# Another set of filler products for TensorE's first warm-up

## The chip, the cores and the metric

The kernel runs on one core of a Trainium2 chip. The metric is the device time of one execution in microseconds (us). TensorE, VectorE, ScalarE and GpSimd (POOL) each work through an instruction list of their own, SyncE (SP) issues transfers, and semaphores tie them together.

## The reference, cut to what matters

Two gated blocks on x of 2 x 512 tokens, 256 features:

```
xn = layernorm(x)
s  = attention(xn @ Wq, xn @ Wk, xn @ Wv) @ Wo      # 16 heads of 16, 4 key/value heads, rotary on half of each head
g  = silu((silu(xn @ Wgate) * (xn @ Wup)) @ Wdown)  # 256 -> 1024 -> 256
x  = x + s * g
xn = layernorm(x)
s  = linear attention of xn (one sum over the tokens of a batch, times the rotated queries) @ W_out + b_out + xn
g  = silu(top-1 mixture of 8 experts, 256 -> 512 -> 256, times the router's probability)
x  = x + s * g
```

The change touches neither block. It concerns what TensorE does before its first useful instruction.

## The kernel before, in words

The tokens stand as eight tiles of 128 rows, four to a batch. The first microseconds are these. SyncE issues the loads: x of batch 0, the first part of the constants (`cst`), the qkv weights, x of batch 1, the gate and up weights (`wgu`, into `shared`), and the rest. VectorE waits for x, computes mean and inverse root for batch 0 and writes its normed tiles (`apply_norm`, L1041); then the same for batch 1. TensorE waits for the constants, runs a filler (`keep_warm`, L1369), and then for each batch transposes eight blocks of 128 x 128 of the normed rows (L1379) and multiplies by the qkv weights (L1390, 384 columns, four tiles times two halves of the features). Between the two ScalarE copies the transposed rows out of PSUM (L851 for batch 0, L877 for batch 1). The copies of the products out of PSUM are L856 and L858.

A gate or up product is made of three fp32r products (L1578): the high part and the remainder of the weights times those of the rows. ScalarE rounds the weights to the high part in four pieces (`round_weights`, L863) and the rows (L867); the remainders are VectorE's, for the first two pieces and batch 0 (L1055, L1062), or GpSimd's (L743). The high part of the first pieces lies in `w_high_words`, a view as fp32r of the buffer `late_weights`. VectorE overwrites the transposed rows of batch 0 with their remainder at L1062, so it waits there until the qkv products of batch 0 are done (`qkv_psum`). After that it rotates and splits the heads (L606 to L624, L1093), and TensorE transposes what results in bf16 (L1453). From there on a list worked out beforehand (`attention_plan`) sets the order of the scores, probabilities, values and gate, up and down products.

`keep_warm(n, bank)` transposes the identity into a PSUM bank that nobody reads. It stands in three places: 18 times here (`WARM_UP`), and 4 and 8 times (`ROWS_WARM`, `TILE_WARM`) ahead of the experts. Nothing but its place in TensorE's list holds it: it waits for the constants, and what stands behind it in the list waits for it.

## Time and profile before

| | us |
|---|---|
| two timed runs | 353.35 and 357.67, median 355.51 |
| the profiled execution | 353.23 |
| its span, first to last instruction | 351.2 |
| mean granted TensorE clock over the span | 0.978 |

The times of the rows are us from the start of the span. A row of a timeline merges neighbouring instructions of one kind: start, length of the whole, engine, line, operation, tiles, shapes, how many, and in brackets the idle time before and what ended it. An instruction of TensorE lasts longer than the distance to the next, since they are pipelined; the distance is what it costs in a row of them. A plain fp32 product has two records, an fp32r, a bf16 product or a transpose one.

### The profile page before, as it was taken

How to read it: one execution, taken by the hardware profiler on the slowest of the kernel's cores; microseconds unless marked ns; L12 is line 12 of the kernel's file. 1: busy time of each engine (PE TensorE's matmuls, PEld its weight loads, DVE VectorE, ACT ScalarE, POOL GpSimd, SP SyncE). 2: the span in 40 equal slices, each digit the busy share in tenths (PEclk: the TensorE clock that was granted, in tenths of full speed). 3: DMA queues.
4: the chain of work that ended last, by engine and by line, in shares of the span. 5: the costliest groups of instructions: out<-in, count | busy, mean ns of one | idle time of the engine just before them, and what ended most of it. 6: DMA issues, size and time to landing. Idle time of an engine off the chain costs nothing.

```text
span 351.2 us, 4689 instructions
## 1 busy us (share of the span) xinstructions
PE 319.4 (91%) x1598; PEld 188.7 (54%) x1598; DVE 230.7 (66%) x489; ACT 155.8 (44%) x282; POOL 67.4 (19%) x72
## 2 busy tenths in 40 slices
PE   3977799999999999999999999998986999999960
PEld 3655565445555544555554555465654566666640
DVE  3997849767575677877957711289995754456631
ACT  1477414676667455553674564411204222323220
POOL 4008650000020000000000000020673000346641
PEclk9999989999999999999999999998998999999997
DMA  7980000000000000000000040059226990424510
GB/s 245 411 218 2 0 1 2 0 4 0 1 3 2 1 0 3 0 0 4 1 2 1 0 167 15 0 216 367 77 97 189 400 424 32 154 89 136 154 51 11
DMA packets 11370, 30.56 MB, mean 87 GB/s; under 512 B 1773, under 2 KB 8014, under 8 KB 10064
## 3 DMA queue, kind: packets, MB, share of 16 engines
q1 hardware_dynamic: 9392, 26.01, 20.4%
q0 software_dynamic: 1952, 4.22, 3.9%
q8 instruction: 15, 0.25, 0.3%
q14 instruction: 11, 0.09, 0.1%
HBM read 27.22 MB, written 6.60 MB: 96 GB/s over the span
## 4 chain that ended last, share of the span: by engine, by line
PE 74%; DVE 14%; issue 3%; DMA 3%; POOL 2%; ACT 2%; DVEq 0%; POOLq 0%
PE ps L1578 11%; PE ps L1523 9%; PE ps L1491 8%; PE ps L1591 8%; PE ps L1513 7%; PE ps L1646 6%; PE ps L1632 5%; PE ps L1654 5%; PE ps L1428 3%; DVE nmax L1103 3%; PE ps L1453 2%; POOL slot_rows L787 2%; PE ps L1407 2%; PE ps L1622 1%; DMA x<-in_x 1%
## 5 line engine op out<-in xcount | busy, mean ns | idle before, releaser
L1103 DVE TENSOR_REDUCE nmax<-ps 128x1 f32<-128x512 f32 x128 | 85.5, 687 | 34.5 <-PE ps L1491 33.8
L907 ACT ACTIVATE shared<-ps 128x512 f32<-128x512 f32 x128 | 74.2, 594 | 53.8 <-PE ps L1513 52.7
L1491 PE MATMUL ps<-experts 96*128 96x512 bf16 x128 | 48.2, 384 | 1.6 <-DVE experts L1110 1.1
L1513 PE MATMUL ps<-experts 99*128 99x512 bf16 x128 | 48.5, 382 | 0.0
L1591 PE MATMUL ps<-shared,experts 128*128 128x256 f32 x128 | 38.0, 386 | 0.0
L1523 PE MATMUL ps<-shared,experts 128*32 128x512 f32 x256 | 34.1, 605 | 0.3 <-ACT shared L907 0.3
L1491 PEld LDWEIGHTS ps<-experts 96*128 96x128 bf16 x128 | 12.5, 98 | 36.7 <-DVE nmax L1103 18.3
L1591 PEld LDWEIGHTS ps<-shared,experts 128*128 128x128 f32 x128 | 23.3, 191 | 9.8 <-issue 3.4
L777 POOL TENSOR_TENSOR experts<-experts,late_weights 128x768 f32<-128x768 f32 x1 | 1.8, 1805 | 130.8 <-ACT experts L897 130.8
L1428 PE MATMUL ps<-late_weights,xnT 128*128 128x512 f32 (+1 forms) x64 | 23.9, 522 | 0.5 <-DVE shared L1069 0.5
L915 ACT ACTIVATE experts<-ps 96x1024 bf16<-96x1024 bf16 x18 | 17.9, 1018 | 11.6 <-PE ps L1453 11.6
L1646 PE MATMUL ps<-experts,xsT 128*128 x44 | 21.4, 610 | 0.7 <-ACT xsT L969 0.7
L1632 PE MATMUL ps<-experts,shared 128*128 x88 | 20.9, 380 | 0.8 <-ACT shared L975 0.8
L1654 PE MATMUL ps<-experts,xsT 128*128 x44 | 20.7, 593 | 0.0
L1578 PE MATMUL ps<-xnT,late_weights 128*128 128x512 f32 x48 | 19.1, 398 | 0.0
L1428 PEld LDWEIGHTS ps<-late_weights,xnT 128*128 128x128 f32 x64 | 12.4, 201 | 10.0 <-issue 8.4
L1513 PEld LDWEIGHTS ps<-experts 99*128 99x128 bf16 x128 | 12.4, 98 | 9.9 <-issue 3.5
L1632 PEld LDWEIGHTS ps<-experts,shared 128*128 128x128 f32 x88 | 15.9, 190 | 2.7 <-issue 1.0
L1162 DVE SCALAR_TENSOR_TENSOR gx<-gated,ps 128x256 f32<-128x256 f32 x8 | 3.4, 421 | 18.5 <-ACT gated L944 18.4
L1578 PE MATMUL ps<-xn,late_weights 128*128 128x512 f32 x24 | 12.7, 527 | 2.3 <-DVE experts L1154 2.2
L935 ACT ACTIVATE tanh_g<-ps 128x512 f32<-128x512 f32 x16 | 9.6, 598 | 11.2 <-PE ps L1578 10.7
L800 POOL DMA_INDIRECT x<-token_rows,xs x6 | 6.2, 1033 | 39.9 <-DMA token_rows<-gx 37.4
(209 smaller groups left out, 526.9 us busy)
## 6 DMA issues: line engine op xcount, KB each, us to landing
experts<-in_experts SPq DMA_DIRECT2D x8, 1536.0 KB, 12.6
shared<-in_wgu SPq DMA_DIRECT2D x1, 2048.0 KB, 11.1
slot_rows<-in_empty SPq DMA_DIRECT2D x1, 1950.0 KB, 19.5
late_weights<-slot_rows SPq DMA_DIRECT2D x9, 130.0 KB, 4.2
x<-in_x SPq DMA_DIRECT2D x2, 512.0 KB, 5.5
shared<-in_wdn SPq DMA_DIRECT2D x1, 1024.0 KB, 13.1
token_rows<-x SPq DMA_DIRECT2D x1, 1024.0 KB, 14.4
token_rows<-gx SPq DMA_DIRECT2D x1, 1024.0 KB, 4.9
```

Of the source, the lines that this page charges most:

```text
L907: nc.scalar.activation(probs[:, n % 2, hh, :], ps[:, 2 + hh % 2, :], ACT.Exp, scale=float(HD) ** -0.5).then_inc(s["exp_done"], 1)
L915: nc.scalar.activation(dst, src.rearrange("p (h s) -> p h s", h=2), ACT.Copy).then_inc(s["misc_free" if b else "stack_copied"], 1)
L1103: nc.vector.tensor_reduce(nmax[:, 4 * t + hh:4 * t + hh + 1], ps[:, m % 2, :], AX, ALU.max, negate=True).then_inc(s["max_done"], 1)
L1428: last = nc.tensor.matmul(bank[:, a, 0:hi - lo], xnT[:, k, P * j:P * j + P], win[:, k, lo:hi], start=k == 0, stop=k == KD - 1)
L1491: nc.tensor.matmul(ps[:, m % 2, :], qs[0:KS, b, GR * g + hh, P * t:P * t + P], ks[0:KS, b, g, :], start=True, stop=True).then_inc(s["score ...
L1513: nc.tensor.matmul(ps[:, 2 + hh % 2, :], ks[0:KM, b, g, P * t:P * t + P], qs[0:KM, b, GR * g + hh, :], start=True, stop=True).then_inc(s[" ...
L1523: last = nc.tensor.matmul(ps[VW * hh:VW * hh + VW, 4, :], vaug[:, TB * b + t, g, :], probs[:, n % 2, hh, :], start=t == 0, stop=t == TB - 1)
L1578: ins = nc.tensor.matmul(ps[:, bk, :], w_parts[w_], x_parts[x_], start=k == 0 and n_ == 0, stop=k == KD - 1 and n_ == 2)
L1591: ins = nc.tensor.matmul(ps[:, bk, 0:D], hT[:, i, P * (j % TB):P * (j % TB) + P], wdn[:, i, :], start=i == 0, stop=i == NI - 1)
L1632: last = nc.tensor.matmul(ps[:, 6, 0:D], hmT[:, i % 2, P * k:P * k + P], Wm[:, bass.ds(base[i] + 2 * KD * EI + D * k, D)], start=k == 0, s ...
L1646: last = nc.tensor.matmul(ps[:, i % 2, :], xsT[:, i % 2, P * k:P * k + P], Wm[:, bass.ds(base[i] + EI * k, EI)], start=k == 0, stop=k == K ...
L1654: last = nc.tensor.matmul(ps[:, 2 + i % 2, :], xsT[:, i % 2, P * k:P * k + P], Wm[:, bass.ds(base[i] + EI * (KD + k), EI)], start=k == 0, ...
```

## The change

The 18 transposes become four. Then TensorE waits for a copy of the first 384 columns of the constants as fp32r, which ScalarE now makes ahead of its first instruction, in the words that later hold the high part of the weights. On this copy TensorE runs products of 384 columns: a pair of halves (rows 0 to 49 and rows 64 to 113 of the array, into banks 6 and 7), or the whole array (bank 7). Four pairs come first, then twice a whole product and a pair, then three times four products of 32 columns of weights each, side by side in the array's columns (plain fp32, 128 columns of moving data, bank 5), and a pair. The last one raises `warmed`, and ScalarE waits for it before it writes the first high part of the weights into the same words. Results are read by nobody.

```diff
-WARM_UP = 18
...
             act.wait_ge(s["const_loaded"], 16)
+            nc.scalar.activation(w_high_words[:, 0:3 * P], cst[:, 0:3 * P], ACT.Copy).then_inc(s["warm_words"], 1)
             nc.scalar.activation(identb[:], ident, ACT.Copy).then_inc(s["identb_ready"], 1)
...
             act.wait_ge(s["wgu_loaded"], 16)
+            act.wait_ge(s["warmed"], 1)
             round_weights(0)
...
             pe.wait_ge(s["const_loaded"], 16)
 
-            keep_warm(WARM_UP, 7)
+            words = w_high_words[:, 0:3 * P]
+
+            def whole_array():
+                return nc.tensor.matmul(ps[:, 7, 0:3 * P], words[:, 0:P], words, start=True, stop=True)
+
+            def two_halves():
+                for half in range(2):
+                    rows = slice(64 * half, 64 * half + 50)
+                    last = nc.tensor.matmul(ps[:, 6 + half, 0:3 * P], words[rows, 0:P], words[rows, :], start=True, stop=True)
+                return last
+
+            def column_groups():
+                for a in range(4):
+                    nc.tensor.matmul(ps[32 * a:32 * a + 32, 5, 0:P], cst[:, 0:32], cst[:, 0:P], start=True, stop=True)
+
+            keep_warm(4, 7)
+            pe.wait_ge(s["warm_words"], 1)
+            for _ in range(4):
+                two_halves()
+            for _ in range(2):
+                whole_array()
+                two_halves()
+            for _ in range(3):
+                column_groups()
+                last = two_halves()
+            last.then_inc(s["warmed"], 1)
             for b in range(B):
```

TensorE's list at its start, before (a name with an arrow is what is written and read; `cst` are the constants, `ps` is PSUM, `wl` the qkv weights, `xn` and `xnT` the normed rows and their transpose):

```order
L1364 UNCONDITIONAL_BRANCH
L1369 MATMUL ps<-cst 128x128 x18
L1379 MATMUL ps<-cst,xn 128x128 x8
L1390 MATMUL ps<-wl,xnT 128x384 x8
L1379 MATMUL ps<-cst,xn 128x128 x8
L1390 MATMUL ps<-wl,xnT 128x384 x8
```

The same place now (`late_weights` is the buffer of the fp32r copy):

```order
L1365 UNCONDITIONAL_BRANCH
L1370 MATMUL ps<-cst 128x128 x4
L1383 MATMUL ps<-late_weights 128x384 x8
L1378 MATMUL ps<-late_weights 128x384
L1383 MATMUL ps<-late_weights 128x384 x2
L1378 MATMUL ps<-late_weights 128x384
L1383 MATMUL ps<-late_weights 128x384 x2
L1388 MATMUL ps<-cst 32x128 x4
L1383 MATMUL ps<-late_weights 128x384 x2
```

The last two rows stand there twice more; then follow the transposes and products of both batches, L1379 and L1390 of before as L1405 and L1416, as they were.

ScalarE's list at its start, before:

```order
L848 ACT_TABLE_LOAD
L848 ACTIVATE identb<-cst 128x128 [waits const_loaded]
L851 ACTIVATE xnT<-ps 128x512 [waits xnT_psum] x2
L863 ACTIVATE late_weights<-shared 128x1024 [waits wgu_loaded]
L863 ACTIVATE late_weights<-shared 128x1024
```

And now:

```order
L847 ACT_TABLE_LOAD
L847 ACTIVATE late_weights<-cst 128x384 [waits const_loaded]
L848 ACTIVATE identb<-cst 128x128
L851 ACTIVATE xnT<-ps 128x512 [waits xnT_psum] x2
L863 ACTIVATE late_weights<-shared 128x1024 [waits warmed,wgu_loaded]
L863 ACTIVATE late_weights<-shared 128x1024
```

One copy stands ahead of that of the identity, and the first rounding of weights waits for one semaphore more.

## Rows read from the trace of the kernel before

**Rows 1.** The page: span, and busy us with share and instructions by engine.
```profile
span 351.2 us, 4689 instructions
PE 319.4 (91%) x1598; PEld 188.7 (54%) x1598; DVE 230.7 (66%) x489; ACT 155.8 (44%) x282; POOL 67.4 (19%) x72
```

**Rows 2.** Chain of waits up to 46 us: start, length, what.
```profile
0.72 4.47 DMA x<-in_x
...
17.39 1.22 DVE shared L1055
18.61 1.20 DVE xnT L1062 x2
19.81 0.73 DVE gx L606
...
27.46 0.34 DVE experts L1093
27.94 1.08 PE ps L1453 x16
```

**Rows 3.** Timeline of VectorE (DVE), 14.9 to 20.5 us.
```profile
14.96 1.38 DVE L1041 TENSOR_SCALAR xn<-x,st 128x256 f32<-128x256 f32 x4
16.25 2.35 DVE L1055 TENSOR_TENSOR shared<-shared,late_weights 128x1024 fp32r<-128x1024 f32 x2
18.52 1.29 DVE L1062 TENSOR_TENSOR xnT<-xnT,xn 128x512 fp32r<-128x512 f32 x2
19.73 0.82 DVE L606 TENSOR_TENSOR gx<-experts,cst 128x640 f32<-128x640 f32 x1
```

**Rows 4.** Timeline of TensorE (PE), 5 to 21 us.
```profile
5.86 4.10 PE L1369 MATMUL ps<-cst 128*128 128x128 f32 x18 [5.86 <-DMA cst<-in_const]
9.91 1.87 PE L1379 MATMUL ps<-cst,xn 128*128 128x128 f32 x8
12.45 5.40 PE L1390 MATMUL ps<-wl,xnT 128*128 128x384 f32 x16 [0.66 <-ACT xnT L851]
17.68 1.04 PE L1379 MATMUL ps<-cst,xn 128*128 128x128 f32 x8
20.49 0.91 PE L1390 MATMUL ps<-wl,xnT 128*128 128x384 f32 x2 [1.77 <-ACT xnT L877]
```

**Rows 5.** Timeline of ScalarE (ACT), 5 to 21 us.
```profile
5.83 0.31 ACT L848 ACTIVATE identb<-cst 128x128 bf16<-128x128 f32 x1 [3.83 <-DMA cst<-in_const]
11.70 1.08 ACT L851 ACTIVATE xnT<-ps 128x512 f32<-128x512 f32 x2 [5.56 <-PE ps L1379]
13.70 2.00 ACT L863 ACTIVATE late_weights<-shared 128x1024 fp32r<-128x1024 f32 x2 [0.91 <-DMA shared<-in_wgu]
17.88 1.30 ACT L856 ACTIVATE experts<-ps 128x640 f32<-128x640 f32 x2 [1.14 <-PE ps L1390]
19.06 0.39 ACT L858 ACTIVATE experts<-ps 128x256 f32<-128x256 f32 x1
```

**Rows 6.** Stretches: length, busy by engine, granted TensorE clock (PEclk), DMA, GB/s.
```profile
core 0: us, PE busy (x) PEld busy (x) DVE busy (x) ACT busy (x) POOL busy (x), PEclk, DMA share, GB/s
9.00:11.00 2.00, 2.00 (x10) 1.61 (x9) 1.90 (x8) 0.00 (x0) 0.00 (x0) 1.00 0.99 426
17.00:19.00 2.00, 1.72 (x11) 1.13 (x9) 2.00 (x3) 1.12 (x2) 0.00 (x0) 1.00 1.08 353
46.00:49.00 3.00, 3.00 (x9) 2.32 (x8) 1.37 (x2) 0.21 (x1) 2.91 (x5) 0.50 0.01 4
268.00:270.00 2.00, 2.00 (x11) 2.00 (x10) 0.22 (x1) 1.57 (x6) 0.00 (x0) 0.50 0.91 241
```

**Rows 7.** Timeline of TensorE, 267 to 271 us.
```profile
268.13 1.91 PE L1369 MATMUL ps<-cst 128*128 128x128 f32 x8
```

**Rows 8.** Groups of TensorE by line, 8 to 9 us, then 11 to 11.6 us.
```profile
L1369 PE MATMUL ps<-cst 128*128 128x128 f32 x7 | 1.7, 421 | 0.0
...
L1379 PE MATMUL ps<-cst,xn 128*128 128x128 f32 x5 | 1.2, 401 | 0.0
```

**Rows 9.** Timeline of TensorE, 47.6 to 50.1 us.
```profile
48.12 0.63 PE L1578 MATMUL ps<-xn 128*128 128x512 f32 x1
48.55 0.63 PE L1578 MATMUL ps<-xnT,xn 128*128 128x512 f32 x1
...
49.50 0.40 PE L1578 MATMUL ps<-xnT,late_weights 128*128 128x512 f32 x1
49.73 0.39 PE L1578 MATMUL ps<-xn,shared 128*128 128x512 f32 x1
```

**Rows 10.** Timeline of TensorE, 65.5 to 68.2 us.
```profile
66.06 0.38 PE L1491 MATMUL ps<-experts 96*128 96x512 bf16 x1
66.28 0.38 PE L1513 MATMUL ps<-experts 99*128 99x512 bf16 x1
66.59 1.06 PE L1523 MATMUL ps<-shared,experts 128*32 128x512 f32 x8
67.59 0.39 PE L1491 MATMUL ps<-experts 96*128 96x512 bf16 x1
```

**Rows 11.** Timeline of all engines, 27 to 32 us.
```profile
27.61 2.40 POOL L743 TENSOR_TENSOR shared<-shared,late_weights 128x1024 fp32r<-128x1024 f32 x1 [22.59 <-DVE experts L624]
...
27.94 1.51 PE L1453 MATMUL ps<-identb,experts 128*96 128x128 bf16 x24 [0.64 <-DVE experts L1093]
```

More of the change, by code:

```diff
@@ L488, in two_gated_blocks @@
         names = ("acol_psum acol_ready act_step attn_T_ready bias_added branch_free branch_psum branch_ready "
-                 "const_loaded cos1 counts down_ready down_tanh dve_step e_down e_gate e_gated e_h e_tanh e_up "
+                 "const_loaded warm_words warmed cos1 counts down_ready down_tanh dve_step e_down e_gate e_gated e_h e_tanh e_up "
                  "early_gate_free early_up_free end_free exp_done experts_here first_part gate_free gate_ready heads_T "
```

## The prediction

> **What bounds the kernel now.** I read the page first for the span, then the timeline of each engine over the first 21 us, which is all that the change touches, then the chain of waits up to 46 us for what sets the pace there, then single stretches for prices. TensorE is busy 91% of the 351.2 us span, so the whole kernel is mostly its own [rows 1]. The start is not. The chain of waits runs over VectorE: it loads x, norms four tiles, norms four more, lowers two pieces of weights (L1055), lowers the rows of batch 0 (L1062), prepares the heads from L606 to L1093, and only at 27.94 hands over to TensorE [rows 2]. From 14.96 to past 20 VectorE's rows follow each other without idle time [rows 3]. In the same time TensorE waits for the constants until 5.86, runs 18 filler transposes until the rows of batch 0 are there, transposes them from 9.91, waits 0.66 for ScalarE's copy, runs the qkv products from 12.45 and is then idle 1.77 [rows 4]. So the start of TensorE has room, and the question is how much.
>
> The room is this. The qkv products end at 17.85; ScalarE's copies of them (L856) begin at 17.88, take 1.30 and are done at 19.18 [rows 5]. VectorE needs these products twice: as leave to overwrite at L1062, which starts at 18.52 only because L1055 ends there, and as copied heads at L606, which starts at 19.73 because L1062 ends there [rows 3]. With the products d later, L1062 moves to 17.9 + d, and L606 to 19.2 + d. The first passes 18.52 at d = 0.6, the second 19.73 at d = 0.5. **Up to 0.5 us of delay costs nothing, and every further part goes one to one into the chain.** A gain on TensorE here gives nothing, since VectorE then starts no row sooner.
>
> The clock needs care. The granted clock is 1.00 in every row of the start, and 1.00 on average at 17 to 19 [rows 6]. But the first 18 transposes take 4.10 us, 0.21 apart as the same transposes at 268, where 0.50 was granted; the eight at 17.68 take 1.04, 0.11 apart [rows 4, 6, 7]. So TensorE ran at 1.2 GHz from 5.86, and the 1.00 there is no record. The last transpose of batch 0 starts at 11.46 (9.91 + 0.27 + 6 x 0.213) and is the first short one: the five around it average 401 ns where the filler has 421, so it took some 320 [rows 8], and the qkv products, 16 records in 5.40, run at 2.4 GHz. **The rise came at about 11.5**, before the products. What was before it is transposes alone. The warm-up of before has done its work in this execution; a better one can't give more than it already has.
>
> Next to this stands a rule of the Trainium skill ("TensorE: Matmul & The Clock Gate", Part 4): transposes don't count as activity of the engine as products do, so the clock doesn't rise in them. The trace speaks against it: it rose behind 26 transposes and nothing else. By the rule the clock would come up sooner in a warm-up of products, which is rival 2, worked out below from rows alone.
>
> **The change, part by part.** All on TensorE's way to the transposes of batch 0, counted at the half level first.
> - It removes 14 of 18 filler transposes. Four remain: 5.86 + 0.05 + 4 x 0.21 = 6.76.
> - It adds a copy on ScalarE, 384 columns, fp32r out. One of 256 columns takes 0.39, two of 512 take 1.08 [rows 5], so 0.5, from 5.83 to 6.33. TensorE's wait for it is over before the four transposes are. Behind it in ScalarE's queue the bf16 identity moves from 5.83 to 6.3; its first reader is TensorE at 27.94 [rows 2]. Nothing.
> - 18 half-array products in nine pairs. An fp32r product of 512 columns takes 0.43 at the half level (48.12 to 48.55) and 0.23 at full [rows 9], so 384 columns take 0.32. No row shows two row halves. The bounds are 0.33 for a pair side by side and 0.64 one after the other. The nearest row is the four column groups: eight records of 512 columns are done in 1.00 us (66.59 to 67.59) [rows 10], where one such plain fp32 record takes 0.43 at full (0.32 for 384 columns [rows 4]). They ran four at a time. I take 0.33: 9 x 0.33 = 2.97.
> - Two whole-array products: 0.64.
> - Three rounds of four column groups, 128 columns, plain fp32, two records each: 2 x 0.21 + 0.02 = 0.45 a round, 1.35.
> - 11 changes of form. Entering the groups costs 0.09: the product before them starts at 66.28, takes 0.22, and they start at 66.59; leaving costs 1.00 - 0.86 - 0.02 = 0.12 [rows 10]. 11 x 0.10 = 1.1. That holds for the halves as an estimate only.
>
> Sum at the half level: 6.76 + 2.97 + 0.64 + 1.35 + 1.1 = 12.8. If the clock rises at 11.5 as before, the 1.3 left (0.3 of it changes of form) shrinks to 0.8: **the filler ends at 12.3, where it ended at 9.75**. VectorE has had the rows ready since 10.8, so the transposes wait for the filler now. They then run at full: ScalarE's first copy can start one change of form, six steps of 0.11 and 0.3 of latency later, at 13.35, where it was 11.70 [rows 5]. d = 1.65, less 0.5 of room: **+1.1 us**. The transposes gain 0.8 from the higher clock, and it is in that.
>
> The Trainium skill ("TensorEngine Tiling (Array Packing)", Tiling Modes, Key Properties) says that a change of tiling mode drains the engine. A full drain would cost what a record lasts beyond its step, 0.2 us at the half level, so 2.2 in place of 1.1, and the end would be 0.8 us later. The row of 0.09 to 0.12 decides.
>
> Other waits. ScalarE now waits for "warmed" ahead of its first rounding of weights. It waits for the weights until 13.70 anyway, and its two copies of batch 0 stand ahead and end at 14.4, past 12.3. So the wait is never last; the rounding is 0.7 late, ends at 16.35 and VectorE's second L1055 needs it at 17.39 [rows 2]. Free. If the filler ran past 14.4, it would still be the transposes behind it that come late. Everything that follows on ScalarE and TensorE for batch 1 shifts by d = 1.65, VectorE by 1.1: TensorE had 0.64 idle ahead of 27.94 [rows 11], more than the difference of 0.5. POOL and SP are not ordered by the change: POOL's first long work waits for L624 of VectorE and shifts with the chain. Nothing after 28 us changes but its time.
>
> Against its own execution (353.23, the span of 351.2 and 2.0 around it) the sum is 354.3. The median of the two timed runs is 2.3 higher, and they are 4.3 apart (353.35 and 357.67), so the trace stands at their lower end. I put the median halfway: 354.3 + 1.1 = **355.4 us**. A measurement can't tell less than about 2%, 7.1 us, from no change.
>
> **The rivals.**
> 1. *The halves run one after the other.* 9 x 0.31 = 2.8 more at the half level, 1.7 after the rise: the filler ends at 14.0, d = 3.3, +2.8: 356.0 on this execution, 357.1 as median. For it: no row of row halves. Against: the column groups overlap.
> 2. *The clock rises sooner.* If products bring it, say, after the first pairs at 8.2, the 4.6 left is 1.0 of changes and 3.6 halved: the filler ends at 11.0, ScalarE copies at 12.05, d = 0.35, inside the room. The time is that of before: 353.2, 354.3 to 355.5 as median. Against: the rise came 5.7 us after the first transpose with the engine at work all the time, and nothing in the trace says that another form brings it sooner. The Trainium skill's sentence on transposes (the page and part above) speaks for it, and the rise in this trace against that sentence.
> 3. *The longer timed run of before is a missed rise, and the change cures it.* The 16 qkv records at half would take 5.2 us more, less 0.5 of room is 4.7, against the 4.3 between the two timed runs. Then every run of the changed kernel is near 354.3 and the median is that. For it: the sizes agree. Against: the clock also fell at 45.7 (0.50 granted from 46 to 49 [rows 6]) and later, and stretches of that kind can come and go as well.
> 4. *Slower.* With gaps at 11 changes of form the clock stays at 1.2 GHz through the filler and rises only in or after the qkv products. The filler then ends at 12.8, the transposes take 1.87, ScalarE copies at 14.6, d = 2.9, and the products add 5.2: +7.6, 360.8 on this execution. It decides from a rise later than about 13; a rise after 21 adds the second set of products and passes 362.6, the 2% mark.
> 5. The change leaves the time alone to the last tenth, because changes of form cost nothing and the pairs overlap: d = 1.0, +0.5. It is the lower edge of my case.
>
> **How the numbers follow.** My case, with rival 5 as its edge, 0.50; rival 1 0.12; rival 2 0.11; rival 3 0.18; rival 4 0.09. My case alone has 354 to 357. The range takes in rivals 2 and 3 on the lower side and rival 1 and the longer runs of my own case on the upper, and leaves most of rival 4 out: 352.9 to 359.2. For over 2% faster, below 348.4, no mechanism here is large enough, since the start holds no 7 us that TensorE could give back: 0.02 for what I don't see. Over 2% slower needs the late form of rival 4: 0.04. Within: 0.94.
>
> **What would show it.** In the changed trace: the four transposes, then the first pair at about 6.85; the two records of a pair some 0.01 apart (0.32 for rival 1); 0.1 of gap at each change; the last filler at 12.3; the first transpose of batch 0 there and not at 9.9; a first record of the clock at 11.5 or sooner; L851 at 13.3, L856 at 19.5, L606 at 20.8, and the first bf16 transposes at 29.0 for 27.94. I am wrong if VectorE's L606 stays at 19.7, if L606 moves and the end doesn't, or if the clock rises behind the qkv products.

## The result: 3% slower, and the profile after

| | us |
|---|---|
| changed kernel, two timed runs | 363.65 and 365.70, median 364.67 |
| kernel before, beside them | 353.35 and 357.67, median 355.51 |
| ratio | 1.030, 95% from 1.024 to 1.037 |
| profiled execution, and its span | 365.7, 363.6 (before 353.23, 351.2) |
| mean granted TensorE clock | 0.969 (before 0.978) |

The ratio and its interval go by the undisturbed runs alone, so 1.030 is not the quotient of the two medians (1.026).

The forecast was 355.4 with a range to 359.2. The time is outside it, and on the side of rival 4.

The page after, span and busy time by engine:

```profile
span 363.6 us, 4751 instructions
PE 328.9 (90%) x1628; PEld 191.5 (53%) x1628; DVE 231.1 (64%) x489; ACT 156.1 (43%) x283; POOL 67.3 (19%) x72
```

The other engines' work is what it was in [rows 1]; TensorE has 30 records and 9.5 us of busy time more. TensorE's start, the timeline from 5 to 27 us (the lines behind the filler are 26 higher now: L1379 is L1405, L1390 is L1416; VectorE's L606 is L605, its L1303 L1304):

```profile
6.11 1.11 PE L1370 MATMUL ps<-cst 128*128 128x128 f32 x4 [6.11 <-DMA cst<-in_const]
7.15 1.65 PE L1383 MATMUL ps<-late_weights 50*128 50x384 f32 x8
8.73 0.69 PE L1378 MATMUL ps<-late_weights 128*128 128x384 f32 x1
9.34 0.69 PE L1383 MATMUL ps<-late_weights 50*128 50x384 f32 x2
...
11.19 0.65 PE L1388 MATMUL ps<-cst 128*32 128x128 f32 x8
11.78 0.69 PE L1383 MATMUL ps<-late_weights 50*128 50x384 f32 x2
...
14.79 1.97 PE L1405 MATMUL ps<-cst,xn 128*128 128x128 f32 x8
17.33 6.91 PE L1416 MATMUL ps<-wl,xnT 128*128 128x384 f32 x16 [0.57 <-ACT xnT L851]
24.07 1.04 PE L1405 MATMUL ps<-cst,xn 128*128 128x128 f32 x8
```

Read the starts, not the lengths. From the whole product at 8.73 to the next pair at 9.34 there are 0.61 us for 0.32 of work, so the change of form costs 0.29. The four pairs in a row of 7.15 take 1.65 in all for eight records: steps of 0.49, 0.32 and 0.32 from pair to pair, and the two records of a pair start 1 to 3 ns apart. The halves do run side by side. The first transpose of batch 0 stands at 14.79, in [rows 4] at 9.91. The eight transposes take 1.97, and the 16 qkv products 6.91 in place of 5.40.

The stretches 17 to 19 and 21 to 23 us (length, busy us and records of each engine, granted clock, share and rate of the transfers):

```profile
17.00:19.00 2.00, 1.67 (x3) 1.10 (x4) 0.36 (x1) 2.00 (x4) 0.00 (x0) 1.00 1.08 339
21.00:23.00 2.00, 2.00 (x8) 1.18 (x7) 0.00 (x1) 0.00 (x0) 0.00 (x0) 1.00 1.09 295
```

The three records of qkv products in the first are 0.64 apart, 1.2 GHz; the eight that the second touches are 0.32 apart, 2.4 GHz. As in the kernel before, the column says 1.00 for both, since the first record of the clock comes at 20.38. **TensorE came up to 2.4 GHz only there, 14.3 us after its first record; before it was 5.7.** VectorE, 15 to 26 us:

```profile
15.20 1.38 DVE L1042 TENSOR_SCALAR xn<-x,st 128x256 f32<-128x256 f32 x4
18.64 2.36 DVE L1056 TENSOR_TENSOR shared<-shared,late_weights 128x1024 fp32r<-128x1024 f32 x2 [2.06 <-ACT late_weights L863]
24.27 1.29 DVE L1063 TENSOR_TENSOR xnT<-xnT,xn 128x512 fp32r<-128x512 f32 x2 [3.27 <-PE ps L1416]
25.60 0.82 DVE L605 TENSOR_TENSOR gx<-experts,cst 128x640 f32<-128x640 f32 x1
```

In [rows 3] these rows had no idle time. Now VectorE waits 2.06 for ScalarE's rounding and 3.27 for the qkv products. ScalarE in the same time:

```profile
6.08 0.52 ACT L847 ACTIVATE late_weights<-cst 128x384 fp32r<-128x384 f32 x1 [4.08 <-DMA cst<-in_const]
6.52 0.29 ACT L848 ACTIVATE identb<-cst 128x128 bf16<-128x128 f32 x1
16.58 1.09 ACT L851 ACTIVATE xnT<-ps 128x512 f32<-128x512 f32 x2 [9.77 <-PE ps L1405]
17.55 2.00 ACT L863 ACTIVATE late_weights<-shared 128x1024 fp32r<-128x1024 f32 x2
24.27 1.30 ACT L856 ACTIVATE experts<-ps 128x640 f32<-128x640 f32 x2 [3.68 <-PE ps L1416]
```

The new copy takes the 0.5 us forecast, and the rounding starts straight behind L851 with no wait of its own, so `warmed` is never last. The chain of waits (start, length, what) was VectorE alone in [rows 2]; it is now the filler:

```profile
6.11 1.11 PE ps L1370 x4
...
14.86 1.70 PE ps L1405 x7
...
17.33 6.92 PE ps L1416 x16
24.27 1.31 ACT experts L856 x2
25.60 0.82 DVE gx L605
...
33.84 1.08 PE ps L1479 x16
```

The first bf16 transposes stand at 33.84, where [rows 2] has 27.94: **5.9 us of the 12.5 between the two profiled executions are lost at the start.** The delay is then carried unchanged to 271 us. Of the rest, 1.9 lies between there and the seventh result of the experts, and 4.7 in the last four intervals between results of the experts' tiles. Before (VectorE's results, the first and the last of five from 319 to 344 us):

```profile
319.91 0.48 DVE L1303 TENSOR_SCALAR late_weights<-ps,late_weights 128x256 f32<-128x256 f32 x1 [1.28 <-PE ps L1632]
...
342.85 0.48 DVE L1303 TENSOR_SCALAR late_weights<-ps,xs 128x256 f32<-128x256 f32 x1 [3.04 <-PE ps L1632]
```

and after (the same two, 327 to 356 us):

```profile
327.66 0.48 DVE L1304 TENSOR_SCALAR late_weights<-ps,late_weights 128x256 f32<-128x256 f32 x1 [1.19 <-issue]
...
355.30 0.48 DVE L1304 TENSOR_SCALAR late_weights<-ps,xs 128x256 f32<-128x256 f32 x1 [2.93 <-PE ps L1658]
```

22.9 us became 27.6. The instructions here are the same. TensorE's rows say where the time is. Before, the first products on the experts' rows at 269.83, those of one of the last tiles at 329.53, and the stretch 270 to 274 us:

```profile
269.83 2.44 PE L1646 MATMUL ps<-experts,xsT 128*128 x4
...
329.53 1.89 PE L1632 MATMUL ps<-experts,shared 128*128 x8
270.00:274.00 4.00, 4.00 (x11) 1.74 (x9) 0.69 (x1) 1.54 (x6) 0.00 (x0) 0.88 0.94 335
```

and after, the same two groups of products and the stretches 276 to 280 and 341 to 345 us:

```profile
276.61 3.50 PE L1672 MATMUL ps<-experts,xsT 128*128 x4
...
340.92 3.50 PE L1658 MATMUL ps<-experts,shared 128*128 x8 [3.07 <-issue]
276.00:280.00 4.00, 4.00 (x9) 1.98 (x8) 0.00 (x0) 1.69 (x7) 0.00 (x0) 0.53 0.89 270
341.00:345.00 4.00, 4.00 (x10) 3.01 (x11) 1.19 (x3) 0.41 (x2) 0.84 (x1) 0.57 0.19 64
```

Matched record by record, TensorE is 5.9 us late up to 271 us and 6.8 behind its wait for the experts' first rows (2.94 us for 2.03). Behind the half level of 276 to 280 it is 7.8 late, ahead of the wait of 3.07 it is 8.2, 11.4 behind that wait, 13.2 behind the products that follow it at the half level, and 12.5 at the end. The wait has the name "issue": the profile shows nothing that TensorE waited for. Two transfers of instructions fall into 337.5 to 341 us; that TensorE waited for them isn't shown. So there were two questions: what holds the clock down at the start, and what the rest is. The rows "start" in the table further down are the first bf16 transposes of each profile, less the 27.94 of before.

### The profile page after: what moved, and what is told of

The parts are those of the page before. It is cut to its first block, busy times and chain, and to the rows that moved or that the text cites. A ratio compares the mean times of both kernels' runs of the same rounds, so it can differ in the third digit from the quotient of the medians.

```text
span 363.6 us, 4751 instructions
## 1 busy us (share of the span) xinstructions
PE 328.9 (90%) x1628; PEld 191.5 (53%) x1628; DVE 231.1 (64%) x489; ACT 156.1 (43%) x283; POOL 67.3 (19%) x72
## 4 chain that ended last, share of the span: by engine, by line
PE 77%; DVE 10%; issue 4%; DMA 3%; POOL 2%; ACT 2%; SPq 0%; DVEq 0%; POOLq 0%
PE ps L1604 11%; PE ps L1549 9%; PE ps L1517 8%; PE ps L1617 8%; PE ps L1539 7%; PE ps L1672 6%; PE ps L1658 5%; PE ps L1680 5%; PE ps L1454 3%; DVE nmax L1104 2%; PE ps L1479 2%; POOL slot_rows L786 2%; PE ps L1416 2%; PE ps L1433 2%; PE ps L1648 1%
## 5 line engine op out<-in xcount | busy, mean ns | idle before, releaser
L1517 PEld LDWEIGHTS ps<-experts 96*128 96x128 bf16 x128 | 12.5, 98 | 36.7 <-DVE nmax L1104 18.3
L1658 PE MATMUL ps<-experts,shared 128*128 x88 | 22.5, 402 | 3.8 <-issue 3.1
L1672 PE MATMUL ps<-experts,xsT 128*128 x44 | 22.8, 643 | 0.7 <-ACT xsT L970 0.7
L1680 PE MATMUL ps<-experts,xsT 128*128 x44 | 20.7, 593 | 0.0
L1658 PEld LDWEIGHTS ps<-experts,shared 128*128 128x128 f32 x88 | 16.7, 200 | 6.3 <-issue 4.3
L1334 DVE SCALAR_TENSOR_TENSOR gated<-tanh_g,ps 128x512 f32<-128x512 f32 x11 | 7.5, 684 | 13.0 <-ACT tanh_g L988 12.3
L982 ACT ACTIVATE late_weights<-late_weights 128x256 f32<-128x256 f32 x11 | 4.6, 417 | 23.6 <-DVE late_weights L1304 20.9
```

The costliest lines, as they stand in the source:

```text
L1517: nc.tensor.matmul(ps[:, m % 2, :], qs[0:KS, b, GR * g + hh, P * t:P * t + P], ks[0:KS, b, g, :], start=True, stop=True).then_inc(s["score ...
L1658: last = nc.tensor.matmul(ps[:, 6, 0:D], hmT[:, i % 2, P * k:P * k + P], Wm[:, bass.ds(base[i] + 2 * KD * EI + D * k, D)], start=k == 0, s ...
L1672: last = nc.tensor.matmul(ps[:, i % 2, :], xsT[:, i % 2, P * k:P * k + P], Wm[:, bass.ds(base[i] + EI * k, EI)], start=k == 0, stop=k == K ...
L1680: last = nc.tensor.matmul(ps[:, 2 + i % 2, :], xsT[:, i % 2, P * k:P * k + P], Wm[:, bass.ds(base[i] + EI * (KD + k), EI)], start=k == 0, ...
```

## The experiments

**Same work, other order (e2) and one form at a time (e1, e3, e4).** e4 has 1608 records of TensorE, the others the 1628 of the changed kernel, and the filler stays in its place.

e1, before with more transposes:

```diff
-WARM_UP = 18
+WARM_UP = 48
```

> The filler of before, 48 transposes instead of 18: as many records of TensorE as the changed kernel has. Theory 'gaps' (the changed filler keeps the clock down because each change of form stops the stream): here is no gap, the clock rises near 11.5 us, the filler ends near 13.8, the first qkv record starts near 15.5 and VectorE's L606 near 22.2, +2.5 us for 19.73. Theory 'length' (a late filler alone explains the start): L606 near 25.6 as in the changed kernel, +5.9. For the rest of the loss: theory 'place of the code' (TensorE's later stall moves with the number of instructions ahead of it) expects the stall of about 3 us between two products of the experts and 3 to 5 us on top; theory 'clock alignment' expects none of it: total +2.5.

Measured: ratio 1.015 (1.006 to 1.023). The clock rose 4.2 us after the first record, the start is 1.9 later.

e2, the changed kernel's products sorted by form:

```diff
             keep_warm(4, 7)
+            for _ in range(3):
+                column_groups()
             pe.wait_ge(s["warm_words"], 1)
-            for _ in range(4):
+            for _ in range(9):
                 two_halves()
             for _ in range(2):
-                whole_array()
-                two_halves()
-            for _ in range(3):
-                column_groups()
-                last = two_halves()
+                last = whole_array()
```

> The same filler products as in the changed kernel, sorted by form: 4 transposes, 3 rounds of column groups, 9 pairs, 2 whole: 3 changes inside and one at most behind, for 12. Theory 'gaps': the filler ends near 12.3 at 1.2 GHz or sooner, the clock rises before the qkv products, L606 at 20.5 to 21.5, +1 to +2 us at the start. Theory 'forms' (products on part of the array don't bring the clock up): no rise before the qkv products, L606 near 23.5, +4.

Measured: ratio 1.008 (1.003 to 1.014). Its TensorE timeline:

```profile
7.19 1.51 PE L1388 MATMUL ps<-cst 128*32 128x128 f32 x24
8.63 2.93 PE L1383 MATMUL ps<-late_weights 50*128 50x384 f32 x18
11.49 0.61 PE L1378 MATMUL ps<-late_weights 128*128 128x384 f32 x2
11.94 1.03 PE L1403 MATMUL ps<-cst,xn 128*128 128x128 f32 x8
13.64 5.40 PE L1414 MATMUL ps<-wl,xnT 128*128 128x384 f32 x16 [0.67 <-ACT xnT L851]
```

Not one product less than in the changed kernel, yet the transposes stand at 11.94 in place of 14.79, they and the qkv products run at 2.4 GHz, and the clock rose 4.9 us after the first record in place of 14.3. The start is 0.7 later than before in place of 5.9. This settles it for the start: the order is the cause, not the products.

e3 and e4, the changed kernel with 22 pairs and with 24 whole products in place of all else:

```diff
-            for _ in range(4):
+            for _ in range(22):
...
+            for _ in range(24):
+                last = whole_array()
```

> 4 transposes, then 22 pairs of half-array products and nothing else: one change of form, as many TensorE records as in the changed kernel. Theory 'gaps': the clock rises near 11.5 to 12, the filler ends near 13, L606 near 21.4, +1.7. Theory 'forms': the filler runs to 14.1 at 1.2 GHz, the rise comes in the qkv products, L606 at 25 or later, +5.5.

> 4 transposes, then 24 whole-array fp32r products of 384 columns: no change of form. Both theories: the clock rises near 11.5 us as behind transposes, the filler ends near 13.1, L606 near 21.5, +1.8. If the rise comes clearly sooner than behind transposes, products count for more than transposes; if L606 is at 25, what matters is neither gaps nor forms.

Measured: e3 a median of 362.95 against 356.51, but its four times go from 355.96 to 363.53 and no ratio could be formed; e4 1.011 (1.007 to 1.015). The clock rose 4.9 and 3.2 us after the first record, so half-filled rows are not what holds it down. The start is 1.9 and 0.8 later, for fillers that would be 7.0 and 7.7 us of pairs and whole products at the half level. But e1 and e4 lose some 3 us more than that, in the part of the kernel that they don't touch. Neither has a change between the whole and a part of the array in its filler, so the second question is not one of forms.

**Does the number of records cost by itself (e5), and do other changes of form do it (e6)?** e5 puts 30 records of 8 columns into the time in which TensorE waits for ScalarE's copy of batch 1:

```diff
+                if b == 1:
+                    for _ in range(15):
+                        nc.tensor.matmul(ps[:, 0, 0:8], ident, ident[:, 0:8], start=True, stop=True)
```

> The kernel before, its filler untouched, and 15 plain fp32 products of 8 columns (30 records of TensorE) in the 1.8 us in which TensorE waits for ScalarE ahead of the second qkv products. Theory 'place of the code': TensorE's stall stays at its 1587th record, which now stands inside a tile of the experts and not at the branch behind the eighth; a second stall of 1 to 2 us comes at the branch; nothing changes at the start (L606 near 19.7), and the end is 3 to 5 us later than before. Theory 'clock alignment' or chance: no stall inside a tile, and the time of before.

Measured: 1.012 (1.005 to 1.020). It wasn't hidden: the tiny products last 3.85 us, not the 1.77 of the gap, and from 20.9 to 27.7 us 0.50 was granted:

```profile
18.11 3.85 PE L1387 MATMUL ps<-cst 128*128 128x8 f32 x30
...
21.82 5.47 PE L1393 MATMUL ps<-wl,xnT 128*128 128x384 f32 x8
```

They start 0.11 us apart, as transposes of 128 columns do at that level, and 0.21 apart once the clock is down. The start moved by 3.4, 1 us less than the time. As a test of the record count it is spoilt; as one of the clock it shows that an engine with rows in its timeline all along can lose it.

e6, before with groups of columns and single transposes in turn:

```diff
-            keep_warm(WARM_UP, 7)
+            keep_warm(3, 7)
+            for _ in range(5):
+                column_groups()
+                keep_warm(1, 7)
```

> A filler of whole-array work only, 48 records, but with changes of form: 3 transposes, then five times four column groups (128 columns, plain fp32) and one transpose, 10 changes. Theory 'gaps': each change costs 0.29 us, the filler ends at 12.6 or later at 1.2 GHz, the clock does not rise before the qkv products begin or only in the transposes of batch 0; L606 above 23. Theory 'halves' (it is the 50-row halves that keep the clock down, together with the gaps): the clock rises near 11 as in the kernels without gaps, L606 near 20.5 to 21.5.

Measured: 1.011 (1.005 to 1.018).

```profile
6.78 0.66 PE L1376 MATMUL ps<-cst 128*32 128x128 f32 x8
7.37 0.48 PE L1369 MATMUL ps<-cst 128*128 128x128 f32 x1
7.78 0.66 PE L1376 MATMUL ps<-cst 128*32 128x128 f32 x8
```

From transpose to groups 0.41 passes for 0.21 of work, from groups to transpose 0.59 for 0.43: changes of 0.16 to 0.20, smaller than behind 384 columns. The clock rose after 6.9 us; with the filler of before it rose after 4.7 to 5.7 (the profiles of before, e5, e11 and e14). So these changes of form delay it a little, by one profile, and not to 14. The start is 1.0 later.

**The changed kernel again (e7), and ten whole products (e8).**

> The changed kernel once more, for a second trace and more times beside the kernel before. Theory 'gaps': the clock rises again only behind the start of the qkv products, L606 above 24, and the stall inside the experts stands at the 1587th record: 361 to 366. Chance: a rise near 11 to 13 us, L606 near 22, 357 to 360.

Measured: 1.029 (1.020 to 1.039), beside 13 runs of before. The first result holds. In its profile (367.20, the longest of its four runs) the clock rose 17.2 us after the first record and the start is 7.2 later. e8:

```diff
-            keep_warm(4, 7)
+            keep_warm(3, 7)
...
+            for _ in range(10):
+                last = whole_array()
```

> A filler as long as that of before, without changes of form and with 5 records fewer: 3 transposes and 10 whole-array fp32r products of 384 columns (3 x 0.21 + 10 x 0.32 = 3.84 us). Both theories on the start: as before, the rise between 9 and 11.6, L606 near 19.7. Theory 'place of the code': no more stall than before, since the 1587th record comes 6 records behind the end of the last full tile's list, at the branch or after it: the time of before, within 2 us.

Measured: 0.998 (0.994 to 1.003). A rise after 3.5 us, sooner than before, brings nothing: VectorE has no use for it, as the room in the prediction said.

**Fewer records (e9), work in the gap at 43 us (e10, e11).** e9 is before with three plain fp32 products (six records) of 384 columns for the 18 transposes. e10 adds two more where TensorE waits before the scores, and so may keep the clock from the fall at 46 [rows 6]; e11 is before with 15 products of 8 columns at that place.

```diff
-            keep_warm(WARM_UP, 7)
+            for _ in range(3):
+                nc.tensor.matmul(ps[:, 7, 0:3 * P], ident, cst[:, 0:3 * P], start=True, stop=True)
...
+                if it == ("max_parts", 0):
+                    pe.wait_ge(*stack_copy(8))
+                    for _ in range(2):
+                        nc.tensor.matmul(ps[:, 4, 0:3 * P], ident, cst[:, 0:3 * P], start=True, stop=True)
```

> The filler of before (3.84 us at 1.2 GHz) as three plain fp32 products of the identity with 384 columns: 6 records for 18, so TensorE's list is 12 records shorter than before. Theory 'length of the list' (the time of the last tiles of the experts, which stand behind branches, grows with what TensorE's list holds ahead of them): the start of before, and the time of before or 1 us less. Theory 'chance' (the last tiles vary by themselves): the time of before, and the five last steps of VectorE's result (L1303) add up to 23 to 29 us in any kernel.

> As e9, and two more such products in the 2.2 us in which TensorE waits at 42 to 44 us and behind which the clock falls to 1.2 GHz for 3.4 us (16 products of 512 columns or parts of them at half speed, 1.7 us lost). If the clock stays up, the end comes 1 to 1.7 us sooner than that of e9: about 353 where before has 354.5. If the window of the fall lies elsewhere, nothing.

> The kernel before with 15 plain fp32 products of 8 columns (30 records, as many as the changed kernel has more) in TensorE's wait at 42 to 44 us, where nothing waits for them. The start is that of before. Theory 'length of the list': 3 to 4 us longer than before, all of it in the last tiles of the experts. Theory 'chance': the time of before within 1 us.

Measured: e9 0.994 (0.989 to 0.999), e10 0.992 (0.988 to 0.997), e11 1.015 (1.007 to 1.023). e10 from 46 to 49:

```profile
46.00:49.00 3.00, 3.00 (x15) 2.42 (x14) 2.06 (x3) 0.25 (x1) 2.96 (x5) 1.00 0.01 3
```

15 records at the full level for 9 at the half in [rows 6]; but e10 is no clearer ahead of before than e9 is, and several kernels without such products showed no fall there in their profiles either. e11 leaves the start where it was (28.00) and still loses 5.3 us. But its products weren't hidden either:

```profile
41.96 3.41 PE L1438 MATMUL ps<-cst 128*128 128x8 f32 x30
45.23 0.66 PE L1582 MATMUL ps<-xn,late_weights 128*128 128x512 f32 x1
```

They last 3.41 us in a gap of 2.24, so the next product starts at 45.23 where before it starts at 44.30, and TensorE is still 0.9 late at 50 us. That much of the 5.3 is no matter of the list's length.

**The changes of form without column groups (e12), then with more records (e15); ten records at 43 us (e14); fewer late filler records (e13, e16).** e12:

```diff
-            for _ in range(4):
-                two_halves()
-            for _ in range(2):
+            for _ in range(6):
                 whole_array()
-                two_halves()
-            for _ in range(3):
-                column_groups()
                 last = two_halves()
```

> 4 transposes, then six times a whole-array product and a pair of halves (22 records, 12 changes of form, no column groups). Each kind alone brought the clock up 3.2 to 4.9 us after the first record. Theory 'gaps': with a change of 0.29 us behind every 0.32 us of products the filler lasts till about 14.2 and the clock rises only in the qkv products, L606 at 24 to 26, 5 us later than before. If the column groups are what kept the clock down in the changed kernel: a rise near 9 to 12, L606 near 21.5.

Measured: 1.016 (1.012 to 1.021).

```profile
6.89 0.67 PE L1378 MATMUL ps<-late_weights 128*128 128x384 f32 x1
7.49 0.69 PE L1383 MATMUL ps<-late_weights 50*128 50x384 f32 x2
...
14.27 1.97 PE L1400 MATMUL ps<-cst,xn 128*128 128x128 f32 x8
16.81 8.47 PE L1411 MATMUL ps<-wl,xnT 128*128 128x384 f32 x16 [0.56 <-ACT xnT L851]
```

Twelve changes of 0.28 to 0.30, no column groups: the clock rose after 16.9 us and the start is 6.9 later. Pairs alone (e3) and whole products alone (e4) do nothing of the kind, so **the changes between them are enough to make the loss at the start**, and the time follows it, 5.7 us for 6.9.

e15 adds 12 of e11's products to e12 (24 records), e14 has five of them (10 records) in the kernel before. e13 is e9 with one product of 256 or 512 columns for each late `keep_warm`, e16 is e10 with the same.

```diff
+                if it == ("max_parts", 0):
+                    pe.wait_ge(*stack_copy(8))
+                    for _ in range(12):
+                        nc.tensor.matmul(ps[:, 4, 0:8], ident, ident[:, 0:8], start=True, stop=True)
...
-            keep_warm(ROWS_WARM, 3)
+            nc.tensor.matmul(ps[:, 3, 0:2 * P], ident, cst[:, 0:2 * P], start=True, stop=True)
...
-            keep_warm(TILE_WARM, 3)
+            nc.tensor.matmul(ps[:, 3, 0:4 * P], ident, cst[:, 0:4 * P], start=True, stop=True)
```

> e12 (pairs and wholes by turns, 1604 records, 6.5 us over before, all of it in the start) with 12 plain fp32 products of 8 columns in TensorE's wait at about 49 us: 1628 records as in the changed kernel. Theory 'length of the list': 3 to 4 us over e12, so 10 over before, as the changed kernel. Theory 'chance': the time of e12 within 1 us.

> The kernel before with 5 plain fp32 products of 8 columns (10 records) in TensorE's wait at 42 to 44 us. Theory 'length of the list': kernels of 1608 records and more lost 1.5 to 7 us beyond their start, those of 1604 and fewer nothing; so here 1 to 4 us over before. Theory 'chance': the time of before within 1 us.

> e9 with the 12 transposes of the two later fillers, ahead of the experts, as two plain fp32 products of 256 and 512 columns (the same time at 1.2 GHz, 4 records for 12: 1578 in all). Theory 'length of the list': the time of e9 or up to 2 us less. Theory 'chance': the time of e9 within 1 us.

> e10 with the later fillers as in e13 (1582 records), as the candidate for the shortest kernel. Both theories: below before by 2 to 3 us as e10 (352.4 where before had 354.8); 'length of the list' allows up to 2 us more.

Measured: e15 1.024 (1.015 to 1.033), e14 1.004 (0.998 to 1.009), e13 0.998 (0.992 to 1.004), e16 0.992 (0.988 to 0.997).

**No filler at all (e17), and nine pairs alone (e18).**

```diff
-WARM_UP = 18
+WARM_UP = 0
...
-            for _ in range(4):
+            for _ in range(9):
```

> The kernel before without the 18 transposes of the first filler. Theory 'gaps': what counts is how long TensorE has worked without a break before the qkv products; here 1.9 us of transposes, a wait of 0.7, then the products, so the clock rises 3 to 7 us into them, between 16 and 19.5 us, L606 is 1.5 to 3.5 later than 19.73, and the time is 1.5 to 3.5 over before: less than the changed filler loses. If it is 6 or more, the filler of the changed kernel is worth no less than none.

> The changed kernel with its nine pairs of halves in a row and without the whole products and the column groups: 4 transposes, 9 pairs, one change of form, 22 records. Theory 'gaps': the filler ends near 10.1, the clock rises between 9.3 and 12.7, L606 near 20, the time of before within 1.5 us. Theory 'forms': no rise before the qkv products, L606 3 us later.

Measured: e17 1.004 (1.000 to 1.008), e18 1.002 (0.997 to 1.007). Without a filler:

```profile
10.09 1.94 PE L1379 MATMUL ps<-cst,xn 128*128 128x128 f32 x8 [10.09 <-DVE xn L1041]
12.60 8.33 PE L1390 MATMUL ps<-wl,xnT 128*128 128x384 f32 x16 [0.56 <-ACT xnT L851]
```

The clock rises in the products here too, but the transposes stand at 10.09 and not at 14.79, and the start is only 2.6 later. **The changed filler is worse than none.** Nine pairs, which are the changed filler's own without what stood between them, are worth what the 18 transposes are: their clock rose after 3.8 us and the start is 0.2 later.

All kernels but e3, which has no ratio, by number of TensorE records in the profile (e12 and e15 have two fewer than their expectations say). "Loss" is the ratio less one times the median of before in the same comparison; "rest" is loss less the shift of the start, which is read from one profile each.

| | records | rise after | start | loss | rest |
|---|---|---|---|---|---|
| e13, e17, e16 | 1578, 1580, 1582 | 5.1, 8.4, 5.2 | 0.0, 2.6, 0.2 | -0.7, 1.3, -2.9 | -0.7, -1.3, -3.1 |
| e9, e10, e8 | 1586, 1590, 1593 | 5.2, 5.3, 3.5 | 0.1, 0.1, 0.2 | -2.1, -2.8, -0.6 | -2.2, -2.8, -0.8 |
| before | 1598 | 5.7 | 0 | 0 | 0 |
| e12, e18 | 1602, 1602 | 16.9, 3.8 | 6.9, 0.2 | 5.7, 0.6 | -1.2, 0.5 |
| e4, e14 | 1608, 1608 | 3.2, 5.3 | 0.8, 0.0 | 4.0, 1.3 | 3.2, 1.3 |
| e15 | 1626 | 13.6 | 5.2 | 8.5 | 3.4 |
| changed, e7 | 1628 | 14.3, 17.2 | 5.9, 7.2 | 10.8, 10.3 | 4.9, 3.1 |
| e1, e2, e6 | 1628 | 4.2, 4.9, 6.9 | 1.9, 0.7, 1.0 | 5.2, 2.9, 4.0 | 3.3, 2.2, 3.0 |
| e5, e11 | 1628 | 4.7, 5.2 | 3.4, 0.1 | 4.4, 5.3 | 1.0, 5.2 |

The rest averages -1.8 below 1598 records (six kernels), 0.9 at 1602 to 1608 (four) and 3.3 at 1626 and 1628 (eight). So 30 records more go with about 3 us more, whatever the products are. That is a pattern found afterwards over all runs; one of its points, e11, holds 0.9 us of plain delay, and its cause isn't shown. Single pairs bear it out weakly: e14 alone can't be told from before, and e15's interval touches that of e12.

The granted clock goes the same way, and the table leaves it out. Over the runs that enter the ratios its mean (which counts the time ahead of the first record as 1.00) is 0.964 to 0.976 in the kernels e1 to e15 of 1608 records and more, 0.974 to 0.981 in those below 1598, and 0.974 to 0.976 in before beside them. It goes with the time in one and the same kernel too: in each of the five comparisons the runs of before with 0.975 or more are 0.7 to 2.7 us shorter on average than its others. The profile of before was at 0.50 for 3.4 us from 267.5, that of the changed kernel for 6.8 from 273.0 and for 3.4 from 341.2. So part of the rest is TensorE at the half level late in the kernel; whether more records bring that about, or something else does both, no run separates.

The other part of the changed kernel's rest, the wait inside a tile that ends with "issue", is no mark of it. (The wait of 2.18 at before's 1587th record stands 12 records from the end, where most profiles have one; these stand earlier.) A wait of 2.1 to 4.4 us further ahead stands in ten of the 20 profiles: ahead of TensorE's 1587th record in the changed kernel, e1 and e3, ahead of the 1583rd to 1595th in e7, e11, e12 and e15, and ahead of the 1539th to 1549th in e10, e16 and e17, the first two of which are the fastest kernels. In e3 and e15 the profile names ScalarE as what ended it, in the other eight nothing. In e5 no such wait stands at the 1587th record, where the theory 'place of the code' wanted it. That theory is out.

The last four intervals of results, my first suspect, don't carry it by themselves. They sum to 22.9 before and 27.6 after, to 29.2 in e1 and 28.0 in e11, but to 23.6 in e5 and 23.0 in e6, and to 27.9 in e10, with e16 the fastest kernel:

```profile
319.71 0.48 DVE L1303 TENSOR_SCALAR late_weights<-ps,late_weights 128x256 f32<-128x256 f32 x1 [1.24 <-PE ps L1637]
...
347.64 0.48 DVE L1303 TENSOR_SCALAR late_weights<-ps,xs 128x256 f32<-128x256 f32 x1 [1.93 <-PE ps L1637]
```

e10's profiled execution was 358.1 where its median is 352.4, so its 27.9 is likely not its usual. Each kernel has one profile, which says little of its mean there.

## Why the prediction was wrong, step by step

- **What failed: "11 x 0.10" for the changes of form.** There are 12, counting the one into the transposes of batch 0, and they cost 2.98 us in all: 8.69 from the filler's start to the first transpose, less 5.70 of streaming (4 transposes 0.90, nine pairs 2.88, two whole 0.64, groups 1.28). Out of transposes or groups they cost 0.13 to 0.14 here, out of fp32r products of 384 columns 0.29. I took the price from a row of bf16 products and groups at 2.4 GHz [rows 10]. The rule that the prediction weighed and set aside, the drain at a change of mode in the Trainium skill ("TensorEngine Tiling (Array Packing)", Tiling Modes, Key Properties), was the better guide: the estimate worked out from it was 0.2, against 0.25 measured on average.
- **What failed: "if the clock rises at 11.5 as before".** It rose at 20.38. The prediction had the mechanism as rival 4, at 9 in 100, with +7.6 and 360.8 on this execution; it decided from a rise later than 13, and that is what came. The start cost 5.9 in place of 7.6: the clock rose within the qkv products, which took 1.5 more and not 5.2, while the transposes stood 2.0 later than the 12.8 of rival 4. That I gave it 0.09 rests on the same small price. e2, e12 and e18 show that the changes between forms are the cause. By what way they are isn't: no run puts idle time of 0.29 us between products of one form, so the idle time and the change itself aren't told apart.
- The delay d of the qkv products was put at 1.65 and is 6.39 (17.84 to 24.23). The missing 4.74: filler 2.5 longer (1.9 of it changes of form, 0.25 a later arrival of the constants, the rest the rise that didn't come), transposes at the half level 0.7, qkv products 1.5.
- **Right: the room.** d = 6.39 less 0.5 is 5.89; L605 moved from 19.73 to 25.60, 5.87, and the first bf16 transposes by 5.90. In e1, d was 2.40 and the start moved 1.9. This was the step on which the whole sum hung, and it held in every kernel that moved the qkv products of batch 0 (e2: d 1.20, 0.7; e12: 7.44, 6.9; e17: 3.08, 2.6). In e5 it is the products of batch 1 that come late, and L606 stays at 19.7.
- Right: pairs side by side (rival 1 is out; the two records of the first pair start 3 ns apart), the groups (1.28 us of streaming for 1.35), the new copy, `warmed` without effect, the identity in bf16 without effect.
- Rivals 2 and 3: the clock does come up sooner in other fillers (3.2 to 4.9 us after the first record in e1 to e4, e8 and e18), and in e8 and e18, which are no longer than before's, it brings nothing, as rival 2 said. Rival 3 has nothing for it: the four profiles with the filler of before show the rise after 4.7 to 5.7 us, and a rise missed in the unprofiled runs isn't seen anywhere. What goes with their spread is the mean granted clock, as said above.
- **What no step had: "Nothing after 28 us changes but its time".** Of some 10.5 us lost, 3 to 5 lie beyond the start. In the profile they are a wait without a visible releaser and products at the half level from 276 and from 341 us. Over the kernels they go with the number of TensorE's records and with the granted clock; the cause stays open. This decided against the 2% bound too: the start alone (5.9 to 7.2) would have been 1.7 to 2.0%.

The best kernels of the study are e10 and e16, 0.992 of before (0.988 to 0.997), with six long filler records in place of 18 short ones and two products more at 43 us. That is 0.8%, less than the 2% bound, but both intervals lie below 1. e9, with the six records alone, has 0.994, so what the two products add isn't told apart.

## What to carry to other kernels

Sort filler and small products by form. A change between whole-array and part-array products is no free switch: price it at the row whose form and length stand just ahead of it, and look in the trace for when the clock then rises. And before costing anything on an engine at the start, find the room of the engine that sets the pace; here it was right to a tenth of a microsecond and told at once that a better warm-up could bring nothing at the start. When a loss is larger than its place explains, read the granted clock of the late stretches as well as that of the changed one.

## What the runs showed of the hardware

- A pair of row halves, 50 rows each with fp32r products of 384 columns, takes 0.32 us at 1.2 GHz, as one whole product does.
- Leaving a single such product or pair for another form takes 0.28 to 0.30 us at 1.2 GHz (after, e12); behind the four pairs in a row it is 0.13, with 0.16 more between the first and the second of them. Leaving transposes or column groups of 128 columns takes 0.13 to 0.20 (after, e6).
- With a change about every 0.6 us TensorE stayed at 1.2 GHz for 13.6 to 17.2 us after its first record (the changed kernel, e7, e12, e15), and for 3.2 to 4.9 with the same or similar products unbroken (e2, e3, e4, e8, e18). Transposes alone bring the clock up too: 4.2 and 5.7 us after the first (e1, before). The rule on transposes in the Trainium skill ("TensorE: Matmul & The Clock Gate", Part 4) isn't borne out here.
- Thirty records of 8 columns in a row took 3.85 us, 0.11 each at 2.4 GHz, which is what a transpose of 128 columns takes, and the clock fell to 0.50 in them, from 20.9 to 27.7 us (e5).
- The same kernel's executions differ by up to 8 us within one comparison (before beside e9: 351.1 to 359.5), and the longer ones have the lower mean granted clock. The stretch of the experts' last tiles took 21.8 (e9) to 29.2 us (e1) over the 20 profiles, with waits of up to 4.4 us inside a tile that nothing in the profile explains (e16).
